# A graph layer on one core: the two destination products of a quad of edge tiles become one

## The reference, cut to what matters

```
def reference(x, src, dst, edge_attr_64, ...weights...):
    # x: 6250 x 64, edge_attr_64: 206250 x 64, src and dst: 206250 node numbers, dst sorted
    msg = concatenate([x[dst], edge_attr_64], axis=1)
    h = relu(msg @ W1a.T + b1a) @ W1b.T + b1b
    sums = segment_sum(h, src, num_segments=6250)
    counts = segment_sum(ones, src, num_segments=6250)
    agg = sums / maximum(counts, 1.0)[:, None]
    z = relu(concatenate([x, agg], axis=1) @ W2a.T + b2a) @ W2b.T + b2b
    out = concatenate([z, x], axis=1) @ Wr.T + br
    return layernorm(x + out)
```

## Time and profile before

| | |
|---|---|
| median of three runs | 1608.92 us |
| profiled execution, its own time | 1609.42 us |
| its span | 1607.3 us |
| mean granted TensorE clock | 0.986 of full |
| TensorE matmuls | 1552.7 us busy, 97% of the span, 13755 matmuls |
| TensorE weight loads | 1276.8 us, 79% |
| VectorE | 1404.1 us, 87% |
| ScalarE | 941.7 us, 59% |
| GpSimd | 1152.0 us, 72% |

### The profile page before, as it was taken

One profiled execution on the slowest core, in us unless ns is written; L12 is line 12 of the kernel. 1 busy time (PEld: TensorE's weight loads), 2 busy tenths in 40 slices (PEclk: granted clock), 3 DMA queues, 4 the chain that ended last, 5 costly groups with the idle time before them and its releaser, 6 DMA issues.

```text
span 1607.3 us, 42297 instructions
## 1 busy us (share of the span) xinstructions
PE 1552.7 (97%) x13755; PEld 1276.8 (79%) x13755; DVE 1404.1 (87%) x3954; ACT 941.7 (59%) x1808; POOL 1152.0 (72%) x929
## 2 busy tenths in 40 slices
PE   9899999999999999999999999999999999995996
PEld 6578878878887888878878887888888888884885
DVE  5599998999999999999999988999999999884885
ACT  2376767767676776767767674555455554563222
POOL 2277777777777777777877788788788877876451
PEclk9899999999999999999999999999999999997998
DMA  8265655656666566556666669889989898866996
GB/s 253 72 168 159 171 157 162 175 156 169 161 164 166 163 160 167 165 163 164 162 163 166 166 167 305 270 273 290 289 278 284 267 296 273 275 174 219 347 370 198
DMA packets 135500, 335.22 MB, mean 209 GB/s; under 512 B 36506, under 2 KB 69565, under 8 KB 129016
## 3 DMA queue, kind: packets, MB, share of 16 engines
q0 software_dynamic: 53184, 224.62, 43.1%
q1 hardware_dynamic: 80740, 102.43, 26.2%
q10 hardware_dynamic: 1364, 5.49, 1.2%
HBM read 212.88 MB, written 119.52 MB: 207 GB/s over the span
## 4 chain that ended last, share of the span: by engine, by line
PE 84%; DMA 5%; DVE 4%; POOL 2%; issue 2%; ACT 1%; SPq 0%; POOLq 0%; DVEq 0%; ACTq 0%
PE HH L523 22%; PE MS L532 18%; PE PA L548 13%; PE PBk L548 13%; PE RK L561 7%; DMA gbuf<-region,idx 4%; PE RK L640 2%; PE RK L645 2%; PE PA L561 2%; PE CK L608 2%; POOL region L1261 1%; DVE OH L1103 1%; PE RK L657 1%; POOL gbuf L1289 1%; DVE M L983 0%
## 5 line engine op out<-in xcount | busy, mean ns | idle before, releaser
L1261 POOL DMA_INDIRECT region<-stg,dest x806 | 1010.5, 1254 | 349.6 <-issue 181.6
L532 PE MATMUL MS<-W,hT 128*128 128x64 f32 x3224 | 507.9, 258 | 1.3 <-DVE T L1117 0.8
L532 PEld LDWEIGHTS MS<-W,hT 128*128 128x128 f32 x3224 | 467.1, 191 | 3.6 <-issue 2.5
L523 PE MATMUL HH<-eab,pw 128*128 128x512 f32 x806 | 434.7, 621 | 3.3 <-ACT hT L782 2.6
L983 DVE TENSOR_SCALAR M<-pos_of,pos 128x384 bf16<-128x384 int16 x1612 | 404.4, 309 | 0.0
L548 PE MATMUL PA<-Z,M 128*128 128x195 bf16 x2418 | 353.9, 254 | 6.5 <-ACT stg L828 2.6
L828 ACT ACTIVATE stg<-PA 120x585 bf16<-120x585 f32 x403 | 266.4, 661 | 156.8 <-PE PA L548 156.3
L548 PE MATMUL PBk<-Z,M 128*128 128x195 bf16 x2418 | 353.9, 254 | 0.2 <-ACT stg L828 0.2
L548 PEld LDWEIGHTS PA<-Z,M 128*128 128x128 bf16 x2418 | 229.1, 106 | 123.9 <-issue 118.9
L782 ACT ACTIVATE hT<-HH 128x512 f32<-128x512 f32 x403 | 240.8, 597 | 137.3 <-PE HH L523 137.3
L828 ACT ACTIVATE stg<-PBk 120x585 bf16<-120x585 f32 x403 | 265.9, 660 | 52.1 <-PE PBk L548 50.3
(11 more groups left out here) (199 smaller groups left out, 1543.3 us busy)
## 6 DMA issues: line engine op xcount, KB each, us to landing
eab<-in_ea SPq DMA_DIRECT2D x201, 256.0 KB
kb<-keyd SPq DMA_DIRECT2D x201, 128.0 KB
pw<-ptab SPq DMA_DIRECT2D x403, 32.0 KB
region<-stg,dest POOLq DMA_INDIRECT x806
gbuf<-in_xt ACTq DMA_DIRECT2D x6, 422.5 KB
ptab<-OH SPq DMA_DIRECT2D x7, 256.0 KB, 3.3
gbuf<-region,idx POOLq DMA_INDIRECT x98, 8.5
eab<-in_xt SPq DMA_DIRECT2D x12, 130.0 KB
```

Of the source, the lines that this page charges most:

```text
L523: e.matmul(HH[:, :], pw[:, q % 4, :], eab[:, c % NB, at_q:at_q + GE], start=True, stop=True).then_inc(s_h, 1)
L532: ins = e.matmul(MS[:, o:o + D], hT[:, q % 2, 128 * j:128 * j + 128], W[:, W_1B:W_1B + D], start=True, stop=True)
L1261: e.indirect_dma_start(region[s], bass.IndirectOffsetOnAxis(ap=dest[:, g:g + 1], axis=0), stw[:, g % NS, :], None).then_inc(s_sc[g % NS], 16)
```

## The change

The two staircases of a quad are laid below each other on one set of 128 partitions (classes of half 0 on partitions 0 to 49, of half 1 on 64 to 113), so that `S` is `[128, 4, 128]` and no longer `[128, 4, 2, 128]`. One matmul a quad then has both staircases as its stationary operand, and a moving operand of six columns: three parts for each half, where the column of half 0 is zero on the upper partitions and that of half 1 on the lower ones. `stair` writes 128 partitions by 240 numbers for a pair of quads, and no longer 50 partitions by 480.

The chain delivers first lines and steps in this shape. The first lines come from two matmuls of 31 columns, one for each half, into partitions 0 to 63 and 64 to 127 (L624 and L625 of the new kernel). The steps come from a difference matrix that is 128 wide and holds the 50 wide one twice, and `chain_steps` multiplies its result by a mask `C_HALF` that clears the half that does not belong to a column. The table of constants `C` grows from 1319 to 1701 columns, and a memset of `S` shrinks from 1024 to 512 columns.

```
-        offs2 = sb("offs2", [CL, 2 * BG, 2], bf16)
+        offs2 = sb("offs2", [128, 2 * BQ, 2], bf16)
-        S = sb("S", [128, 4, 2, 128], bf16)
+        S = sb("S", [128, 4, 128], bf16)
...
-                            e.matmul(RK[0:CL, Q_OFF:Q_OFF + BG], tri50[:, :], kcb[:, :], start=True, stop=True)
+                            e.matmul(RK[0:64, Q_OFF:Q_OFF + BQ], tri50[:, :], kcb[:, 0::2], start=True, stop=True)
+                            e.matmul(RK[64:128, Q_OFF:Q_OFF + BQ], tri50[:, :], kcb[:, 1::2], start=True, stop=True)
...
-                            e.matmul(RK[0:CL, Q_OFF:Q_OFF + BG], C[0:CL, C_DIFF:C_DIFF + CL], dd[:, 2, :],
+                            e.matmul(RK[:, Q_OFF:Q_OFF + BG], C[0:CL, C_DIFF2:C_DIFF2 + 128], dd[:, 2, :],
                                      start=True, stop=False)
-                            last = e.matmul(RK[0:CL, Q_OFF:Q_OFF + BG], C[0:1, C_ID:C_ID + CL],
+                            last = e.matmul(RK[:, Q_OFF:Q_OFF + BG], C[0:1, C_FIRST:C_FIRST + 128],
                                             C[0:1, C_ROT:C_ROT + BG], start=False, stop=True)
...
-                            for g in range(2):
-                                k = 2 * (q % BQ) + g
-                                at_g = Q_DEST + 3 * ((2 * q + g) % 8)
-                                last = e.matmul(RK[:, at_g:at_g + 3], S[:, q % 4, g, :],
-                                                Dzb[:, b % 2, :, 2 * k + 1], start=True, stop=True)
+                            k = 4 * (q % BQ)
+                            at_q = Q_DEST + 6 * (q % 4)
+                            last = e.matmul(RK[:, at_q:at_q + 6].rearrange("p (k g) -> p k g", g=2), S[:, q % 4, :],
+                                            Dzb[:, b % 2, :, k + 1:k + 4:2], start=True, stop=True)
...
-                        link(e.tensor_copy(Dz[0:CL, b % 2, 0, :], RK[0:CL, Q_OFF:Q_OFF + BG]))
+                        link(e.tensor_tensor(Dz[:, b % 2, 0, :], RK[:, Q_OFF:Q_OFF + BG], C[:, C_HALF:C_HALF + BG],
+                                             ALU.mult))
...
-                        q, n = 2 * m, 2 * of_pair(m)
+                        q, n = 2 * m, of_pair(m)
...
-                        e.tensor_tensor(S[0:CL, q % 4:q % 4 + of_pair(m), :, 0:KC].rearrange(
-                                            "p q g (n u) -> p (q g) n u", u=2),
+                        e.tensor_tensor(S[:, q % 4:q % 4 + n, 0:KC].rearrange("p q (n u) -> p q n u", u=2),
                                         iotab[:, :].rearrange("p (n u) -> p n u", u=2)[:, None, :, :].to_broadcast(
-                                            [CL, n, KC // 2, 2]),
-                                        offs2[:, k:k + n, None, :].to_broadcast([CL, n, KC // 2, 2]),
+                                            [128, n, KC // 2, 2]),
+                                        offs2[:, k:k + n, None, :].to_broadcast([128, n, KC // 2, 2]),
                                         ALU.is_ge).then_inc(s_S, 1)
...
-                        e.tensor_reduce(dsum[:, c % 2, 0:n], RK[0:KC, Q_DEST:Q_DEST + 3 * n].rearrange("p (g k) -> p g k", k=3),
+                        e.tensor_reduce(dsum[:, c % 2, 0:n].rearrange("p (q g) -> p q g", g=2),
+                                        RK[0:KC, Q_DEST:Q_DEST + 3 * n].rearrange("p (q k g) -> p q g k", k=3, g=2),
                                         AX.X, ALU.add).then_inc(s_tail, 1)
```

More of the change, by code:

```diff
@@ L67 @@
     0, 128, 256, 320, 448, 576, 640, 768, 769, 770, 771, 835)
-C_ID, C_MID, C_ID2, C_CLS, C_IOTA, C_ROT, C_DIFF, C_ROWX, C_TRI, C_TRI50, C_SEL, C_LANE, C_ONES, C_P64, C_KT, C_14P, C_DC, C_NEVER, C_TAIL, C_EPS, C_TWO, C_ROWB, C_RUNB, C_DCB, C_CAPS, C_ALL = (
-    0, 128, 192, 320, 370, 490, 552, 602, 651, 779, 829, 891, 1019, 1147, 1148, 1149, 1150, 1151, 1152, 1166, 1168, 1266, 1315, 1316, 1317, 1319)
+C_ID, C_MID, C_ID2, C_CLS, C_IOTA, C_ROT, C_DIFF, C_ROWX, C_TRI, C_TRI50, C_SEL, C_LANE, C_ONES, C_P64, C_KT, C_14P, C_DC, C_NEVER, C_TAIL, C_EPS, C_TWO, C_ROWB, C_RUNB, C_DCB, C_CAPS, C_DIFF2, C_HALF, C_FIRST, C_TRI64, C_ALL = (
+    0, 128, 192, 320, 370, 490, 552, 602, 651, 779, 829, 891, 1019, 1147, 1148, 1149, 1150, 1151, 1152, 1166, 1168, 1266, 1315, 1316, 1317, 1319, 1447, 1509, 1637, 1701)
 C_ROW, C_RUN, C_DEP, C_TAILS = (C_ROWX, C_ROWB), (C_14P, C_RUNB), (C_DC, C_DCB), (C_TAIL, C_TAIL + TAIL[0])
@@ L102, in program @@
         oneb = sb("oneb", [128, 128], bf16)
-        tri50 = sb("tri50", [CL, CL], bf16)
+        tri50 = sb("tri50", [CL, 64], bf16)
         sel = sb("sel", [128, BQ], bf16)
@@ L108, in program @@
         clsb = sb("clsb", [128, CL], bf16)
-        iotab = sb("iotab", [CL, KC], bf16)
+        iotab = sb("iotab", [128, KC], bf16)
         laneb = sb("laneb", [128, 128], bf16)
@@ L289, in _ @@
                 e.memset(state[:, :], 1.0)
-                e.memset(S[:, :, :, :], 0.0)
+                e.memset(S[:, :, :], 0.0)
                 e.memset(Dz[:, :, :, :], 0.0)
@@ L321, in _ @@
                 e.tensor_copy(trib[:, :], C[:, C_TRI:C_TRI + 128])
-                e.tensor_copy(tri50[:, :], C[0:CL, C_TRI50:C_TRI50 + CL])
+                e.tensor_copy(tri50[:, :], C[0:CL, C_TRI64:C_TRI64 + 64])
                 e.tensor_copy(sel[:, :], C[:, C_SEL:C_SEL + BQ])
@@ L327, in _ @@
                 e.tensor_copy(clsb[:, :], C[:, C_CLS:C_CLS + CL])
-                e.tensor_copy(iotab[:, :], C[0:CL, C_IOTA:C_IOTA + KC])
+                e.tensor_copy(iotab[:, :], C[:, C_IOTA:C_IOTA + KC])
                 e.tensor_copy(laneb[:, :], C[:, C_LANE:C_LANE + 128])
@@ L628, in rank @@
                                 last = e.matmul(RK[0:BQ, Q_OFT + CL * g:Q_OFT + CL * g + CL],
-                                                kcb[:, g::2], tri50[:, :], start=True, stop=True)
+                                                kcb[:, g::2], tri50[:, 0:CL], start=True, stop=True)
                         b = block_at(i, 7)
@@ L998, in chain_places @@
                         first = carry[:, s:s + 1] if b == SEGB[s] else run_in[:, (b - 1) % 2, BG - 1:BG]
-                        link(e.tensor_copy(offs2[:, BG * (b % 2):BG * (b % 2) + BG, :],
-                                           RK[0:CL, Q_OFF:Q_OFF + BG, None].to_broadcast([CL, BG, 2])))
+                        link(e.tensor_copy(offs2[:, BQ * (b % 2):BQ * (b % 2) + BQ, :],
+                                           RK[:, Q_OFF:Q_OFF + BQ, None].to_broadcast([128, BQ, 2])))
                         link(e.tensor_copy(BS[0:BQ, b % 2, :, :, :], RK[0:BQ, Q_OFT:Q_OFT + 2 * CL].rearrange(
@@ L1311, in constants @@
     c[:, C_ROT:C_ROT + BG] = 128.0 * (np.arange(BG) % NROT)
-    c[0:CL, C_DIFF:C_DIFF + CL] = np.eye(CL) - np.eye(CL, k=1)
+    for half in range(2):
+        c[0:CL, C_DIFF2 + 64 * half:C_DIFF2 + 64 * half + CL] = np.eye(CL) - np.eye(CL, k=1)
+        c[64 * half:64 * half + CL, C_HALF + half:C_HALF + BG:2] = 1.0
+        c[0, C_FIRST + 64 * half] = 1.0
     for s in range(NSEG):
@@ L1321, in constants @@
     c[:, C_TRI:C_TRI + 128] = np.triu(np.ones((128, 128)), 1) + BIG * np.eye(128)
+    c[0:CL, C_TRI64:C_TRI64 + 64] = np.triu(np.ones((CL, 64)), 1)
     c[0:CL, C_TRI50:C_TRI50 + CL] = np.triu(np.ones((CL, CL)), 1)
```

6 lines of the change are left out of this document (3 added, 3 removed).

## The result

The changed kernel took 1595.16 us (median of 5 runs, 1592.89 to 1598.66), the kernel before in its 5 runs 1606.7 us (1605.31 to 1609.6). The ratio is 0.9918, with a 95% interval of 0.990 to 0.9936. The forecast of 1599 us against the 1608.92 us shown was a ratio of 0.9938, just outside that interval: the direction was right and the gain too small. The measured ratio makes 13.2 us (10.3 to 16.1) where 10.1 were forecast.

What follows compares the result with a forecast made beforehand. TensorE's row of starts was taken to bound the kernel from about 70 to 1450 us. Terms -11.6 - 1.3 + 0.5 + 1.3 + 1.0 = -10.1 us gave 1599 us, range for 8 in 10 from 1594 to 1604.5.

Steps and rivals of the forecast that it cites:

- the one on GpSimd: After the last quad: only GpSimd's last eight scatters are its own; TensorE's earlier gain arrives whole; no term in the sum.
- The removed matmul: In each of 403 quads, one matmul fewer saves TensorE 0.0287 us: 11.6 us gained, bounds 10 and 14.
- the shorter staircase: On VectorE, 26 us less work, gaining time only where TensorE waited: 1.3 us, bounds 0 and 6.2.
- First lines: In the chain, 13 times, one more small matmul at 0.04 us: 0.5 us added, at most 1.8.
- Steps: In the chain, L633 and L635 at 128 wide cost 0.10 us more a block: 1.3 us added, at most 2.0.
- The table: At the start, the larger table of constants lands later and moves everything: 1.0 us added, bounds 0 and 2.7.
- 1, no gain in the second segment: DMA gathers set the second segment's pace, so its 124 quads gain nothing: 1603 us; chance 0.11.
- 2, the weight load as the price of a small matmul: TensorE's load port sets the pace, so a quad saves some 0.1 us: 1569 us; chance 0.02.
- 3: Added terms at upper bounds and a half-clock stretch in the last stage eat most of the gain: 1607 us; chance 0.07.
- 4: In the last stage the granted clock stays at half for a quarter or more: 1610 us and above; chance 0.03.
- 5, six columns at the price of two matmuls: In each quad the one matmul costs what two did, leaving only the added terms: 1610 us; chance 0.01.
- The signs set: L657's line about half; two-quad turn 0.06 us shorter; L634/L636 0.55 to 0.62 us; VectorE's wait +15 to 25 us.

Runs made afterwards that it cites:

- a2: The changed kernel with the one destination product of each quad issued twice into the same columns; 1604.27 us, ratio to before 0.9971.
- a4: The changed kernel with the staircase written twice (128x480), giving VectorE its old load, TensorE keeping the single product; 1597.75 us, ratio to before 0.9929.
- d4: The changed kernel with a small memset of an unread tile behind each of GpSimd's 806 scatters; 1764.43 us beside 1798.24 us of before.
- series d: Follow-up series with the changed kernel again and three variants; the kernel before, timed again in it, took 1798.24 us.
- a3: The kernel before with only the table of constants padded from 1319 to 1701 columns; ratio to before 0.9995.
- b2: The kernel before with the steps' two f32 matmuls on a stationary operand 128 wide; 1818.1 us, with before at 1815.04 us.
- c4: The same kernel as b2, run again in another series; 1794.11 us, with before at 1799.96 us.
- the changed family: In the scatter figures, the changed kernel, a2 and a4; 1595.16, 1604.27 and 1597.75 us.
- series a: First follow-up series, on the kernel before and the changed kernel with single alterations; the kernel before took 1609.69 us in it.
- b to e: The four later follow-up series, with variants of both kernels; the kernel before, timed again in each, took 1798 to 1815 us.

## What held of the prediction, and the step that failed

The direction, the bound and the main mechanism were right: TensorE's row of starts sets the time, and a2 gives two thirds of the gain back by nothing but a second small matmul. The size was not. The forecast gain was 10.1 us: 11.1 from the row and 1.0 lost to the table. The row gave about 7 (10.2 behind L657 less 3.2 for the steps), and over 4 us more came at the seam and behind it, for which the prediction had no term. That the two errors partly cancelled is luck.

**The step that failed** is the one on GpSimd. I had read it at 75 to 77% busy, looked at its waits only behind the last quad, and wrote that what TensorE gains before arrives whole; so GpSimd's part stood in the sum at nothing. The runs showed 2.3 us at the seam beyond what the row gave there (2.83 less 0.53 behind L657), and 2.1 us from 300 to 402 (4.04 less 2.66 behind L657, plus 0.73 for the steps).

The share of 76% leaves out the 0.30 us that GpSimd spends ahead of every scatter. With it, GpSimd was taken for 94% of the stretch from 10 to 280 before and for 88% after; it was nearly full, though not quite, and waited for evictions for some 43 us net. Then, from quad 250 on, five further scatters of zeros are put between the others in both kernels. At quad 256 a scatter began 7 us behind the end of its eviction, before and after. With little room GpSimd works off such a delay slowly. Averaged over quads 276 to 283 it was still 3.65 us behind in all three traces of before, 1.87 us in the changed kernel, 0.81 in a2 and 0.70 in a4. The first gather stands behind those scatters, and is issued 23.58 us behind hidden 280 in the three of before and 21.74, 20.48 and 20.13 us in the others, which follows the delay. Before and after:

```profile
957.50 0.99 POOL L1261 DMA_INDIRECT region<-stg,dest  x1 [0.30 <-issue]
958.80 1.03 POOL L1261 DMA_INDIRECT region<-stg,dest  x1 [0.30 <-issue]
960.13 1.16 POOL L1261 DMA_INDIRECT region<-stg,dest  x1 [0.30 <-issue]
961.60 1.44 POOL L1280 DMA_INDIRECT gbuf<-region,idx  x1 [0.30 <-issue]
```

```profile
951.97 1.09 POOL L1262 DMA_INDIRECT region<-stg,dest  x1 [0.30 <-issue]
953.37 1.01 POOL L1262 DMA_INDIRECT region<-stg,dest  x1 [0.30 <-issue]
954.68 1.35 POOL L1262 DMA_INDIRECT region<-stg,dest  x1 [0.30 <-issue]
956.34 1.40 POOL L1281 DMA_INDIRECT gbuf<-region,idx  x1 [0.30 <-issue]
```

ScalarE waits in its own order of work for the gather to land (L807), its next eviction comes late by that, and TensorE's permute waits for the eviction. Before, then after:

```profile
970.63 0.26 ACT L807 ACTIVATE ids<-gbuf 128x60 bf16<-128x60 bf16 x1 [4.13 <-DMA gbuf<-region,idx]
971.59 0.72 PE L548 MATMUL PA<-Z,M 128*128 128x195 bf16 x6 [1.63 <-ACT stg L828]
```

```profile
965.66 0.26 ACT L807 ACTIVATE ids<-gbuf 128x60 bf16<-128x60 bf16 x1 [2.79 <-DMA gbuf<-region,idx]
966.61 0.72 PE L548 MATMUL PA<-Z,M 128*128 128x195 bf16 x6 [0.34 <-ACT stg L828]
```

This wait of TensorE was 1.6, 1.8 and 3.5 us in the three traces of before, 0.3 and 0.4 us in the changed kernel and a2, and none in a4. The chain of waits can be read in the traces, but no run made GpSimd's scatters shorter or longer by themselves where it had a full queue; d4 was to do so and ran in series d, without such a queue. So the seam's gain is argued and not shown. The landing has a part of its own: a3's gather took 1.9 us longer from issue to use than that of the first trace, and its seam is the longest. From 300 to 402 the distances behind `hidden` fell by 1.7 us; there no run takes the causes apart.

**The removed matmul and the shorter staircase**, -11.6 and -1.3 us, were over by 2.7 us together. Over the whole run the distances behind L657 add up to 30.14 us before and 19.89 after, 10.2 us for both. They can't be parted cleanly, since the order of taking them away matters. From 10 to 280 the product is worth 4.65 us with the long staircase (before against a4, 19.19 and 14.54 behind L657) and 5.79 us with the short one (a2, 18.22 and 12.43), which is 0.017 to 0.021 us a quad and 6.9 to 8.6 us for 403. The staircase is worth 1.0 to 2.4 us there. The distance between two L657 is 0.029 us as read. But behind the last of them the mean distance from 10 to 280 is 0.042 us before and 0.046 us after, where the median over the run is below 0.03: in some turns TensorE waits there, and then an earlier end only lengthens the wait. A distance in a full row is an upper bound. The staircase's rule (one saving for each of 13 blocks) was too narrow for this reason.

**First lines**, +0.5 us: nothing. L624 and L625 of the changed kernel start together, and three matmuls stand where two stood. Against the earlier trace rows:

```profile
415.97 0.20 PE L624 MATMUL RK<-kcb,tri 50*64 50x31 bf16 x1
415.97 0.20 PE L625 MATMUL RK<-kcb,tri 50*64 50x31 bf16 x1
416.02 0.19 PE L626 MATMUL RK<-kcb,tri 50*50 50x62 bf16 x1
416.13 0.21 PE L627 MATMUL RK<-rotb,oneb 1*50 1x62 bf16 x1
```

From the first to the rotation's matmul 0.16 us, as before. The step from one half of the partitions to the other thus cost nothing that shows. In the Trainium skill, TensorEngine Tiling (Array Packing), section Key Properties, it is a change of tiling mode that drains the engine and not one of tile alone, and the trace agrees.

**Steps**, +1.3 us, at most 2.0: 13 x 0.245 = 3.2 us, as read from the distances in the changed kernel, b2 and c4. This bound was wrong. I took L662 and L669 as the nearest rows and counted their successors' distances, which had moving operands of 49 and 1 columns and other neighbours. What changed with the operand's width is the load: a load of L633 took 120 ns at the median and one of L634 184 ns, and each of the four starts got about 0.06 us longer. In the Trainium skill, TensorE: Matmul & The Clock Gate, section LDWEIGHTS (loading the stationary operand), a load takes its columns divided by 1.2 in ns, whatever the rows. By an estimate from that page 78 more columns are 0.065 us and four loads 0.26 us, and the trace agrees with 0.245. That page would have given the right term.

**The table**, +1.0 us: L348 began at 11.66 us and not 11.25, 0.4 us, which is within what traces differ by; the pairs of the later series have 0.6 to 1.25 us for 318 columns. So the term's sign holds, and its size is known only to within a microsecond. The rest of the +1.45 us in the first column goes with the clock, as far as can be told: 10.2 us at half clock in three stretches between 42 and 70 us in before, 13.6 us in the changed kernel. The last column's 3.5 us are mostly the clock too: a3, which like the changed kernel lacks the half clock behind 1485 us, is 2.3 us shorter there than the first trace of before.

**The rivals.** 1, no gain in the second segment: refuted, it gained more a quad than the first. 2, the weight load as the price of a small matmul: refuted by a2. 3 and 4 did not come. 5, six columns at the price of two matmuls: refuted by the timeline and a2.

**The signs set.** The matmul's own time and count (403) and the staircase's 0.28 us came as said, TensorE stayed above 99%, and C landed 9.6 us after its issue. Four came otherwise. The line L657 covers 28.90 us in 540 us where it covered 33.46, 14% less and not half, because one matmul's own 0.168 us is counted in full; the sign was reckoned wrongly. A turn of two quads got 0.036 us shorter on average from 10 to 280, not 0.06. L634 and L636 took 0.72 us, not 0.55 to 0.62. VectorE's wait for L657 grew by 6 us only,

```profile
DVE pos L988 <- PE RK L657: 89.6, 165, 4.1
```

and not by 15 to 25. A part of the difference went into other instructions of VectorE that got longer: L961 836 ns after 795, L983 315 after 309 on 1612 of them, together some 18 us. The distance from L657 to its successor, which was not to exceed 0.04 us, has over the run a median of 0.028 us and a mean of 0.049; the mean was 0.045 before, so that sign could not have decided.

## What to carry to other kernels

Where an engine's row is full, a removed instruction is worth the distance of starts at most; take the waits behind it off. Add the issue time ahead of each scatter to GpSimd's busy share before calling it free (76% became 94% here), and look at how far its work is behind wherever one segment hands over to the next. For a wider stationary operand in f32 count the columns of every load, once for each of the two matmuls that the trace shows.

## What the runs showed of the hardware that was not expected

- A scatter on GpSimd takes from 0.99 to 4.2 us; by its place in a round of eight the mean goes from 1.12 to 1.72 us in before. The mean over all stays within 3 ns over three traces of one order of work (1253, 1254, 1256), and was 1147 to 1167 ns in the three of the changed family.
- Two bf16 matmuls on 50 rows that write to different halves of the partitions start within 0.01 us of each other, in all 13 blocks.
- The same program took 1607 to 1610 us at first and in series a, and 1798 to 1815 us in b to e. The last stage took 145 to 151 us in all of them, the turns with quads some 10 to 17% more in b to e. The granted clock was 1.00 for most of both, but in b to e 24 to 106 us of the turns with quads ran at 0.50, in short stretches, where the others had at most 3.4 us; that is at most 53 us of loss and doesn't account for all of the difference.
